# Attention over tiles: 782 gathered tiles a layer, copied to 830 slots by SyncE, in a two-layer graph network

## The reference

```
h = relu(layernorm(x)); x = x + rgcn(rgcn(h))        # out[dst] += W[rel] @ h[src]; + h @ loop_w + bias; relu
h = relu(layernorm(x))
for l in (1, 2):                                     # edges and one self loop for each node, 4 heads of 32
    xw = h @ W                                       # al_s, al_d = xw . a_src, xw . a_dst, per head
    e = leaky_relu(al_s[src] + al_d[dst], 0.2)
    alpha = softmax of e over the edges of one dst
    h = elu(batchnorm(segment_sum(alpha * xw[src], dst) + b))
x = x + h
```

## Time and profile before

| | |
|---|---|
| median of 3 runs | 5504.15 us (5494.9 to 5508.55) |
| span of the profiled execution, first to last instruction | 4547.9 us |
| own time of the profiled execution | not listed; median minus span is 956.25 us |
| busy: PE, PEld, DVE, ACT, POOL | 69%, 50%, 56%, 24%, 69% |
| POOL instructions | 3271, of them 1564 gathers by tile and 1660 by slot |

### The profile page before, as it was taken

One profiled execution on the slowest core, in us unless ns is written; L12 is line 12 of the kernel. 1 busy time (PEld: TensorE's weight loads), 2 busy tenths in 40 slices (PEclk: granted clock), 3 DMA queues, 4 the chain that ended last, 5 costly groups with the idle time before them and its releaser, 6 DMA issues.

```text
span 4547.9 us, 63220 instructions
## 1 busy us (share of the span) xinstructions
PE 3121.2 (69%) x13439; PEld 2273.6 (50%) x13439; DVE 2544.8 (56%) x9924; ACT 1107.5 (24%) x2623; POOL 3132.4 (69%) x3271
## 2 busy tenths in 40 slices
PE   7976777777756666666646676767674666676766
PEld 3444444444434444444435555656563555565655
DVE  6534444444434455555556566767674667676776
ACT  3311222222200111111122233323332223332333
POOL 1057777777767777777677777777727777777772
PEclk9966889888855555555555566656665556665666
DMA  6633444444432222222222222222212222222222
GB/s 232 259 111 98 151 148 154 149 150 154 154 97 62 65 65 65 66 66 66 61 54 54 54 54 54 54 54 54 54 39 58 55 55 55 55 54 54 54 55 73
DMA packets 168049, 394.03 MB, mean 87 GB/s; under 512 B 57414, under 2 KB 92036, under 8 KB 150532
## 3 DMA queue, kind: packets, MB, share of 16 engines
q0 software_dynamic: 103616, 215.16, 17.9%
q10 hardware_dynamic: 37536, 102.42, 6.0%
q1 hardware_dynamic: 26532, 72.39, 4.3%
HBM read 229.57 MB, written 160.17 MB: 86 GB/s over the span
## 4 chain that ended last, share of the span: by engine, by line
PE 39%; DMA 15%; DVE 14%; issue 13%; POOL 11%; ACT 4%; DVEq 2%; SPq 1%; ACTq 0%; POOLq 0%
DMA Gr<-Ttab,GID 12%; PE B L1837 11%; PE B L1979 8%; POOL Gr L2098 8%; PE B L1737 6%; PE B L1799 3%; POOL Gr L2081 3%; DMA Gr<-Gtab,SRC 3%; DVE XA L1128 2%; DVE XA L935 2%; DVE Sr L1027 2%; PE B L1911 1%; PE B L1895 1%; ACT hold L1534 1%; DVE Gr L1103 1%
## 5 line engine op out<-in xcount | busy, mean ns | idle before, releaser
L2098 POOL DMA_INDIRECT Gr<-Gtab,SRC x1660 | 1603.1, 966 | 584.2 <-issue 448.5
L2081 POOL DMA_INDIRECT Gr<-Ttab,GID x1564 | 1497.3, 957 | 604.6 <-PE B L1837 272.8
L1837 PE MATMUL B<-Gr,Sr 128*128 x3328 | 999.0, 410 | 596.5 <-SPq L2114 328.6
L1837 PEld LDWEIGHTS B<-Gr,Sr 128*128 128x128 f32 x3328 | 731.3, 270 | 1051.9 <-issue 1036.4
L1979 PE MATMUL B<-Gr,Sr 128*128 128x136 f32 x3328 | 959.3, 432 | 132.9 <-DVE XA L1128 80.9
L1979 PEld LDWEIGHTS B<-Gr,Sr 128*128 128x128 f32 x3328 | 740.3, 295 | 203.7 <-DVE XA L1128 130.3
L935 DVE TENSOR_TENSOR XA<-XA,B 128x128 f32 x1664 | 471.6, 283 | 571.8 <-PE B L1837 521.3
L1128 DVE TENSOR_TENSOR XA<-XA,B 128x136 f32 x1664 | 480.8, 289 | 294.2 <-PE B L1979 237.9
L924 DVE TENSOR_SCALAR Sr<-iota,DL 128x128 f32<-128x128 f32 x1664 | 493.3, 300 | 20.6 <-issue 16.2
L1737 PE MATMUL B<-XA,H 128*128 128x512 f32 x664 | 412.5, 709 | 1.7 <-DVE H L602 0.4
L1027 DVE TENSOR_SCALAR Sr<-iota,DL 128x128 f32<-128x128 f32 x1664 | 370.2, 295 | 0.0
(11 more groups left out here) (287 smaller groups left out, 3001.2 us busy)
## 6 DMA issues: line engine op xcount, KB each, us to landing
Ttab<-Sr ACTq DMA_DIRECT2D x83, 1024.0 KB, 4.2
Ttab<-Sr SPq DMA_DIRECT2D x51, 1024.0 KB, 3.9
Gr<-Gtab,SRC POOLq DMA_INDIRECT x1660
Gr<-Ttab,GID POOLq DMA_INDIRECT x1564
Gtab<-Gr ACTq DMA_DIRECT2D x83, 66.0 KB
X1D<-Gr ACTq DMA_DIRECT2D x83, 64.0 KB
out<-Sr SPq DMA_DIRECT2D x12, 256.0 KB
Gtab<-XA SPq DMA_DIRECT2D x5, 528.0 KB, 3.8
```

Source lines behind the costliest of these rows:

```text
L1837: e.matmul(B[banks[s % len(banks)]][:, 0:P], selr(s), Gr[:, bass.ds(o, P)], start=True, stop=True).then_inc(slot_mm, 1)
L2081: e.indirect_dma_start(out=Gr[:, (sn + 1) % TG * P:((sn + 1) % TG + 1) * P], out_offset=None, in_=Tt[L][:, :], in_offset=bass.IndirectOffs ...
L2098: e.indirect_dma_start(out=Gr[:, (s % GR) * CW:(s % GR) * CW + 132], out_offset=None, in_=T2[L][0:NPAD][:, :], in_offset=bass.IndirectOffs ...
```

## The change

The attention layers gather tiles too: 782 a layer, into a ring of 64 tiles of 132 columns behind the slots (TILES, in Gr). The slot ring shrinks from 96 to 64. SyncE copies tile to slot, 830 times a layer, by a DMA from SBUF to SBUF whose source address comes from a register (`to_slots`). GpSimd counts landings for SyncE four tiles at a time (TQ): before it issues tile 4g + 3 it waits for tiles 4g - 4 to 4g - 1 and adds 4 to `landed[2 + L]`. It also waits, before tile t, for the copy of slot t - 16, so that a ring place is free. Everything that waited for a slot's gather waits for its copy (`spread`). In the relational layers TensorE's wait on the count stands against max(count, 1), which is one register operation more for each slot. The table SRC is now GID shifted right by 4, one VectorE instruction by tile, in place of matmuls and copies by slot. Buffers move (rows in ROWS, DST used for scratch, ar and pen dropped); VectorE scales OFT by 132/128 once before the attention.

```diff
-GR = 96
+GR = 64
+TW = 132
+TQ = 4
+NTQ = 8
...
-        Gr = sb("Gr", [P, GR * CW])
+        Gr = sb("Gr", [P, GR * CW + TG * TW])
...
+        def wait_tiles(e, L, g):
+            e.wait_ge(tiles[L][g % NTQ], 16 * TQ * (g // NTQ) + 16 * min(TQ, NG - TQ * g))
+
+        def wait_spread(e, n):
+            e.wait_ge(spread[n % NSG], 16 * (n // NSG + 1))
...
+            e.wait_ge(ta.sem, ta.at("gid1"))
+            then(e.tensor_scalar(out=SRC[:, :], in0=GID[:, 0:NT], scalar1=4, scalar2=None, op0=ALU.arith_shift_right), "src")
...
+            e.tensor_scalar(out=OFT, in0=OFT, scalar1=TW / P, scalar2=None, op0=ALU.mult).then_inc(late, 1)
...
-                for n in range(n0 + NSG, min(n0 + 2 * NSG, 2 * NG + (L + 1) * NGS)):
-                    wait_gather(e, n)
+                for n in range(end - NSG, end):
+                    wait_spread(e, n)
...
-            yield from select("src", [f3(spb[2]), f3(spb[3])], (ta, "oft1"), (tv, "tl1"))
...
-                        e.wait_ge(landed[L], kregs[s % 32 // 16][s % 16])
+                        e.reg_alu(kreg, kregs[s % 32 // 16][s % 16], 1, ALU.max)
+                        e.wait_ge(landed[L], kreg)
...
-                for s in range(NGS):
-                    n = 2 * NG + L * NGS + s
-                    wait_gather(e, n - NSG)
-                    if s >= GR:
-                        e.wait_ge(gat_mm, L * NS + s - GR + 1)
+                for t in range(NG):
+                    g = t // TQ
+
+                    if t % TQ == TQ - 1 and g:
+                        wait_tiles(e, L, g - 1)
+                        e.sem_inc(landed[2 + L], TQ)
+
+                    back = t - TG + NGS - NG
+                    if back >= 0:
+                        wait_spread(e, L * NGS + back)
                     e.indirect_dma_start(
-                        out=Gr[:, (s % GR) * CW:(s % GR) * CW + 132], out_offset=None, in_=T2[L][0:NPAD][:, :],
-                        in_offset=bass.IndirectOffsetOnAxis(ap=SRC[:, s:s + 1], axis=0)).then_inc(gat[n % NSG], 16)
+                        out=TILES[:, (t + 1) % TG * TW:((t + 1) % TG + 1) * TW], out_offset=None, in_=T2[L][0:NPAD][:, :],
+                        in_offset=bass.IndirectOffsetOnAxis(ap=SRC[:, t:t + 1], axis=0)).then_inc(tiles[L][g % NTQ], 16)
+                for g in range((NG + 1) // TQ - 1, -(-NG // TQ)):
+                    wait_tiles(e, L, g)
+                    e.sem_inc(landed[2 + L], TQ)
...
+        def to_slots(e, L, kreg, kregs, oregs):
+
+            for s in range(NGS):
+                n = L * NGS + s
+                if s % 16 == 0:
+                    e.reg_load(kregs, TIX[:, s:s + 16])
+                    e.reg_load(oregs, OFT[0:1, s:s + 16])
+                if n >= NSG:
+                    wait_spread(e, n - NSG)
+                if s >= GR:
+                    e.wait_ge(gat_mm, L * NS + s - GR + 1)
+                e.reg_alu(kreg, kregs[s % 16], 1, ALU.max)
+                e.wait_ge(landed[2 + L], kreg)
+                o = off(e, oregs[s % 16], (TG - 1) * TW)
+                e.dma_start(Gr[:, s % GR * CW:s % GR * CW + TW], TILES[:, bass.ds(o, TW)]).then_inc(spread[n % NSG], 16)
...
             rest(e, rest2_store, "r2s")
+            e.wait_ge(rest_done, 2)
+            e.wait_ge(late, 6)
+            to_slots(e, 0, kreg, kregs, oregs)
             for w0, w1 in STORED:
...
+            e.wait_ge(pr_mm, NPAIR)
+            to_slots(e, 1, kreg, kregs, oregs)
```

More of the change, by code:

```diff
@@ L45 @@
 XC = 16
+NST = 33
 SG = 8
@@ L154, in build @@
         H = sb("H", [P, 4, P])
-        lw = [sb(f"lw{l}", [P, P]) for l in range(2)]
+        lwp = [sb(f"lw{l}", [P, P + (1 if l == 0 else 0)]) for l in range(2)]
+        lw, pen = [x[:, 0:P] for x in lwp], lwp[0][:, 0:129]
         rb = [sb(f"rb{l}", [P, P]) for l in range(2)]
@@ L209, in build @@
         built_v = sem("selection_made")
-        landed = [sem(f"landed{l}") for l in range(2)]
+        landed = [sem(f"landed{l}") for l in range(4)]
+        tiles = [[sem(f"tiles{l}_{i}") for i in range(NTQ)] for l in range(2)]
+        spread = [sem(f"spread{i}") for i in range(NSG)]
         slot_mm, slot_add = sem("slot_products"), sem("slot_added")
@@ L298, in build @@
         a3w = A3[:, :].rearrange("p (w k h) -> p w k h", k=3, h=4)
-        art = [ar[:, k, :].rearrange("p (w h) -> p w h", h=4) for k in range(2)]
+        art = [GID[:, k * 4 * NW:(k + 1) * 4 * NW].bitcast(f32).rearrange("p (w h) -> p w h", h=4) for k in range(2)]
         OT = Gr[:, 0:NPAD]
@@ L656, in tables_vector @@
                 yield
-            for k, (src_i, src_f) in enumerate(((fdi, dF), (fsi, sF))):
-                if k:
-                    after("tl0")
-                then(e.tensor_scalar(out=spi, in0=src_i, scalar1=7, scalar2=7, op0=ALU.arith_shift_right, op1=ALU.arith_shift_left), f"ti{k}")
-                yield
-                after(f"ti{k}")
-                then(e.tensor_copy(spb[2 * k], spi), f"th{k}")
-                after(f"th{k}")
-                then(e.tensor_tensor(spb[2 * k + 1], src_f, spb[2 * k], ALU.subtract), f"tl{k}")
-                yield
+            then(e.tensor_scalar(out=spi, in0=fdi, scalar1=7, scalar2=7, op0=ALU.arith_shift_right, op1=ALU.arith_shift_left), "ti0")
+            yield
+            after("ti0")
+            then(e.tensor_copy(spb[0], spi), "th0")
+            after("th0")
+            then(e.tensor_tensor(spb[1], dF, spb[0], ALU.subtract), "tl0")
+            yield
+            yield
+            yield
             then(e.tensor_copy(lb, lF), "lb")
@@ L740, in tables_vector @@
             yield "early"
-            for _ in range(5):
+            e.wait_ge(ta.sem, ta.at("gid1"))
+            then(e.tensor_scalar(out=SRC[:, :], in0=GID[:, 0:NT], scalar1=4, scalar2=None, op0=ALU.arith_shift_right), "src")
+            for _ in range(3):
                 yield
@@ L990, in gat_vector @@
             if L == 0:
-                e.wait_ge(late, 5)
+                e.wait_ge(late, 6)
             else:
@@ L1506, in prep @@
                 c0 = c * CH
-                n0 = 2 * NG + L * NGS + c0
+                end = (L * NGS) + min(c0 + CH, NGS)
                 def then(ins, name):
```

77 lines of the change are left out of this document (39 added, 38 removed).

## The result

| | before | changed | ratio, 95% interval |
|---|---|---|---|
| the comparison that was forecast | 5499.89 us, 4 runs | 5582.23 us, 4 runs | 1.015 (1.0137 to 1.0163) |

The changed kernel is 82 us slower. The forecast was 5378, within 5345 to 5440, and faster with a chance of 0.85; it was wrong in size and in sign.

The account below looks back on a forecast made before the run. POOL's count of gathers was taken to pace all four stages. Terms -122 + 8 + 2 + 1 - 1 = -112 gave a span of 4436 us; the median forecast was 5378 us, between 5392 and 5364, range 5345 to 5440.

Parts of the forecast that it names:

- From span to median: Whole kernel: 956.25 us outside the span, either fixed (5392) or on gathers (5364); the middle, 5378 us, was taken.
- the price of the copies: SyncE in attention: 0.66 us a slot against a supply of one in 1.19 us, so it keeps up.
- Fewer gathers: Attention layers: 782 gathers in place of 830 a layer, 61.3 + 60.7 = 122.0 us less.
- GpSimd's counts and waits: Attention layers: added counts hide in the 0.30 us gap and waits for landings and copies have slack: 0.
- SyncE: Attention copies: issue 0.34 to 0.36 us, with register operations, waits and loads 0.66 us a slot; it keeps up.
- Ends: End of each attention layer: 2.5 + 1.0 + 3.9 = 7.4 us after the last gather's start; +8 for both layers.
- als: Start of each attention chunk's preparation: still waits for data in most chunks, 0 to 8 us.
- TensorE's register operation: Relational layers: 73 to 85 us of queue time, covered by waits for landings; +1, or +10 without cover.
- The tables: SRC's matmuls and copies beside the first relational gathers go: 0; three VectorE operations before them go: -1.
- Rival 1: Attention: copies on the shared DMA engines make landings late and POOL waits; at 6 us landings +375, 5753; chance 8%.
- Rival 2: Attention: chunks become the bound if their work grows 5 to 10% or copies land late; +60, 5435; chance 12%.
- Rivals 3 and 4: Relational TensorE register operation costs 0.1 to 0.2 us a slot, +20 to +80, 6%; attention gather gap grows to 0.37, 5490, 4%.

Follow-up runs that it names:

- g1: Kernel before with TensorE's relational register operation plus 1660 SyncE copies inside SBUF that nobody waits for, late session: 5661.37 us, ratio 1.0186 to the kernel before.
- e2: Kernel before with only TensorE's register operation max(count, 1) ahead of each of 1664 relational slots: 4553.26 us, ratio 1.0 (0.999 to 1.0009).
- g3: Changed kernel with GpSimd counting landings a group later, in a late session: 5628.31 us, ratio 1.0114 to the kernel before.
- a0: Changed kernel as it is, in a prompt session: 4441.59 us against 4555.52 for the kernel before, ratio 0.975.
- e6: Kernel before with the register operation and 830 SyncE copies a layer, 128 x 128, that nobody waits for, prompt session: 4555.4 us, ratio 1.0001.
- h2: Kernel before with 1660 SyncE copies of 16 partitions x 128 columns that nobody waits for, prompt session: ratio within 0.0003 of 1.

## Why the prediction was wrong

**The step that failed is "From span to median".** It put the 956.25 us between the span and the median either into a fixed part or on the gathers, "Nothing in the rows decides; I take the middle". There is no such part: own time less span is 1.7 us. The 956 us lay inside the stages, in waits, in executions of another kind than the one I had the trace of. (The kernel before was not traced in a late session. Its form with eight register operations, 30 us longer, was: span 5601.4, own time 5603.28.) With them goes the sentence on which all the rest stood, that POOL's count of gathers sets the pace of all four stages. It does where the kernel takes 4555 us (als waits for data in all 52 chunks of the trace before, and in 34 of the changed kernel, 237 us in all). In the late traces als waits 0 to 9 us in all, the chunks set the pace, and GpSimd stops in the relational layers too.

**The second step is the price of the copies, "it keeps up, and it was idle before".** In late sessions 1660 copies that nobody waits for cost 102 us (g1). The rest of the change, taken as the difference to that run, gives 38 us back, where the sum had 112. 102 - 38 gives the 63 us by which the changed kernel is slower in that session, but only because the 38 was found by taking it away: that its own copies cost what idle ones do is assumed, not measured. In the comparison it was 82. That the gathers are worth less because the chunks bound is what the ends of the stages show; it was not priced in a late session by itself, and neither was the ring of 64 without slower slots.

**The sum, term by term, in prompt sessions**, where it can be checked:
- Fewer gathers: -122.0 forecast. First to last 999.96 and 987.52 us, 997 and 988 forecast; 98 gathers alone gave -122 and -126. Right.
- GpSimd's counts and waits at 0: the gap stays 0.30 us, longest 0.6. Right. Counting a group later gives a ratio of 0.9749 for 0.975, no difference.
- SyncE: the issue of a copy takes 507 ns where I took 340 to 360 from the stores, and copies that wait for nothing follow each other 0.77 us apart (3276.85 to 3280.72, five steps); with the loads as forecast 0.91 us a slot where I had 0.66. It keeps up with 1.19 all the same.
- Ends: 3282.66 - 3275.18 = 7.5 us, 7.4 forecast, and that is luck. The sum was 2.5 for the landing and 1.0 for two copies and 3.9 for the last copy's landing. In the trace it is 3.3 to GpSimd's last count (3278.46), 2.3 to the issue of the last copy, which stands behind others 0.77 us apart, and 1.8 to its landing. The median landing is 2.0 us, over the 932 copies whose landings are all in the trace. The estimate of 2.2 us by the Trainium skill (DMA: Bandwidth & Descriptors, Anatomy of one DMA — SWDGE path) was the better price of a landing, and its sum for the end, 5.7, fails by the copies in the queue. The other layer's 8.0 us are no landing: als started there without idle time.
- als: it waits up to 16.1 us, where the forecast had 0 to 8 (and the earlier trace rows reach 10.64, not 10.5).
- TensorE's register operation: 0, within 5 us by the interval (e2). The tables were not run by themselves.
- Sum: 4555.52 - 4441.59 = 114 us for 112, and a span of 4441.1 for 4436. The gathers' term carries it; the ends' term came out by two errors that cancel.

**The rivals.** Rival 1 in its own form (landings late, GpSimd stopped) stands in the waits, 543.6 us of L2116 for copies, but counting later changed nothing (g3): SyncE's own waits (L2149) put them down to TensorE's room, hence to the late chunks. The landings of the relational gathers, which the expectation of g1 calls late, are not. Its other half, that DMAs beside the gathers cost time, is what happened in late sessions; a fuller set of DMA engines is not the reason, since the share of 0.40 cost nothing in a prompt session and in late ones it is only 0.33 or 0.34. Rival 2, the chunks become the bound, is the state that I had at 12%, priced for a growth of 5 to 10% of a chunk and so never beyond +60. Rivals 3 and 4 fell.

**Still open:** what makes TensorE's counts late. One rival is untested, the recording of the events itself: of the same changed kernel the prompt trace (a0) holds 96416 rises of counts and the late one 34837, while for the first 260 us they hold 2208 and 2224. Whether that goes with the lateness as its cause or its consequence no run tells. Open too is what of a copy (rows, bytes, or the completion of a DMA as such) it is that costs then, and why the shorter slot ring helps there. The version with a ring of 64 and slower slots beat the kernel before in a late session by 0.4%; the changed kernel beats it by 2.5% in a prompt one. No version was found that beats both kernels in both.

## What to carry to other kernels

Before a sum is made on a trace, its span has to be set against the timed runs. If the two differ by more than the few us around a span, the trace is of another execution than the one that will be measured, and which engine bounds must be doubted before any term is worked out; the range then has to hold "the gain is off the path" as a case of its own. A DMA that nobody waits for is not free by that alone: 1660 such copies cost nothing in one kind of session and 102 us in the other, so such a price is to be taken in both. And a shorter stream of gathers is worth its full price only while the consumer's first instruction of a chunk (als here) is seen waiting for it.

## What the runs showed of the hardware

- The same program took 4555 or 5500 to 5573 us, each within 0.3%, by session and not by chip. In the late kind the first 260 us, ahead of the gathers, hold the same work as in the other (PE 222.94 and 223.38 us, DVE 143.00 and 142.81, the first gather at 260.7 and 261.6); after that TensorE's counts come late: from a slot's matmul to VectorE's addition in the second relational layer 1.94 us in the median and over 9.6 for one in ten, where it is 0.16 and 1.48 otherwise. Gathers' landings don't: 2.56 and 2.50 us.
- 1660 copies of 64 KB inside SBUF: +0.2 us (interval through 0) in one kind of session, +102 us in the other. From issue to landing they take 1.8 us in the median, 66 KB ones 2.0 (prompt).
- Issuing a copy with a source address from a register took 507 ns of SyncE's queue (median), copies with fixed addresses 465 (128 partitions, e6) and 507 (16 partitions, h2); a store to memory took 360. That the register costs anything is not shown.
- Register operations on TensorE ahead of a matmul: 3328 more in the relational layers cost nothing in a prompt session; 13280 in the attention layers 30 us in a late session, 2.3 ns each.
